# Gated cross-attention and a routed mixture of experts: the second group's experts chosen before the fourth group is mixed, and the fourth group's variances raised after the eighth scatter

## The reference, cut to what matters

```python
x = x + tanh(g_xattn) * (0.6 * sigmoid(si[:, :, None] + sj[:, None, :] + b) + 0.4 * layernorm(x))

xf = layernorm(x).reshape(-1, 256)
scores = sigmoid(xf @ w_router)                  # 32 experts in 8 groups of 4
sfc = scores + corr_bias
group_scores = top_k(sfc.reshape(T, 8, 4), 2)[0].sum(-1)
# the best 4 of the 8 groups are kept, and in them the best 6 experts
combine = scores at those 6 experts, else 0
g, u = xf @ gate_w[e], xf @ up_w[e]              # inner width 176
eo = (silu(g) * u) @ down_w[e]
routed = sum over e of combine[:, e] * eo[e]
shared = silu(xf @ sh_gate_w) * (xf @ sh_up_w) @ sh_down_w
x = x + tanh(g_ffn) * (routed + shared)
```

## Time and profile before

| | |
|---|---|
| median of 3 runs | 255.59 us (254.35 to 256.19) |
| span of the profiled execution | 256.1 us |
| TensorE matmul busy | 220.1 us (86%) |
| TensorE weight load busy | 172.2 us (67%) |
| VectorE busy | 130.3 us (51%) |
| ScalarE busy | 79.8 us (31%) |
| GpSimd busy | 147.0 us (57%) |
| moved by DMA | 53.32 MB, 208 GB/s over the span |
| chain that ended last | TensorE 69%, VectorE 13%, DMA 11% |

### The profile page before, as it was taken

How to read it: one execution, slowest core, us unless ns; L and a number is a source line. 1 busy time by engine, 2 the same in 40 slices (tenths; PEclk the granted TensorE clock), 3 DMA queues, 4 the chain that set the end, 5 groups by cost and what they waited for, 6 DMA issues and landing times.

```text
span 256.1 us, 5045 instructions
## 1 busy us (share of the span) xinstructions
PE 220.1 (86%) x1043; PEld 172.2 (67%) x1044; DVE 130.3 (51%) x528; ACT 79.8 (31%) x222; POOL 147.0 (57%) x139
## 2 busy tenths in 40 slices
PE   6896899996899986999999999999999998996000
PEld 5886687884667754877787777778777776774000
DVE  2598768989545542434444534444443443443344
ACT  3607022020011222343434344344444433433000
POOL 6226557777777742564675657656575665465500
PEclk9659599999799999999999999999999999999555
DMA  6999999999999989899785658767677675357787
GB/s 194 274 295 275 408 405 332 243 327 331 320 355 337 385 230 359 179 230 238 140 144 104 114 95 161 115 117 116 103 123 107 113 109 89 42 62 139 157 215 248
DMA packets 41016, 53.32 MB, mean 208 GB/s; under 512 B 5134, under 2 KB 35438, under 8 KB 40998
## 3 DMA queue, kind: packets, MB, share of 16 engines
q1 hardware_dynamic: 24944, 30.40, 40.3%
q0 software_dynamic: 11280, 17.99, 35.5%
q10 hardware_dynamic: 4774, 4.74, 7.1%
HBM read 31.72 MB, written 21.40 MB: 207 GB/s over the span
## 4 chain that ended last, share of the span: by engine, by line
PE 69%; DVE 13%; DMA 11%; issue 3%; POOL 1%; ACTq 1%; ACT 1%; SPq 0%; POOLq 0%
PE pG L734 25%; PE pY L748 17%; PE pG L673 5%; PE pX L728 5%; DMA sum_dram<-xnT,idx 5%; PE pH L742 4%; PE pG L757 4%; DMA xg<-rows_dram 3%; PE pY L684 3%; PE pY L776 3%; DMA given<-in_L_xattn_b_dram 2%; DMA wgu<-sum_dram 2%; PE pX L614 1%; DVE xs L900 1%; DVE rows L894 1%
## 5 line engine op out<-in xcount | busy, mean ns | idle before, releaser
L435 POOL DMA_INDIRECT sum_dram<-xnT,idx x56 | 87.1, 1556 | 61.6 <-ACT xnT L549 36.3
L734 PE MATMUL pG<-wgu,sdown 128*128 x224 | 76.1, 462 | 1.6 <-issue 1.1
L423 POOL DMA_INDIRECT rows_dram<-rows,row_i x48 | 47.2, 983 | 19.0 <-issue 13.8
L748 PE MATMUL pY<-wd,sup 88*128 x224 | 57.5, 379 | 0.0
L1122 DVE COPY sup<-pH 88x256 f32<-88x256 f32 x56 | 23.5, 420 | 58.0 <-PE pH L742 58.0
L734 PEld LDWEIGHTS pG<-wgu,sdown 128*128 128x128 f32 x224 | 38.4, 191 | 14.6 <-issue 2.6
L549 ACT ACTIVATE xnT<-pY,wt 128x256 f32<-128x256 f32 x56 | 26.6, 474 | 57.2 <-PE pY L748 24.7
L748 PEld LDWEIGHTS pY<-wd,sup 88*128 88x128 f32 x224 | 38.0, 190 | 3.2 <-issue 0.2
L742 PEld LDWEIGHTS pH<-ident,sgate 128*88 128x88 f32 x112 | 17.8, 161 | 13.6 <-issue 0.5
L542 ACT ACTIVATE sgate<-pG 128x176 f32<-128x176 f32 x56 | 17.8, 317 | 25.1 <-PE pG L734 24.6
L537 ACT ACTIVATE sdown<-pX 128x256 f32<-128x256 f32 x56 | 21.0, 377 | 7.4 <-PE pX L728 4.5
(11 more groups left out here) (181 smaller groups left out, 236.3 us busy)
## 6 DMA issues: line engine op xcount, KB each, us to landing
wgu<-in_L_ffn_gate_w_dram SPq DMA_DIRECT2D x8, 704.0 KB, 11.0
wgu<-in_L_ffn_up_w_dram SPq DMA_DIRECT2D x8, 704.0 KB, 11.7
wd<-in_L_ffn_down_w_dram SPq DMA_DIRECT2D x8, 640.0 KB
sum_dram<-zeros POOLq DMA_DIRECT2D x3, 1152.0 KB, 13.6
wgu<-sum_dram SPq DMA_DIRECT2D x12, 256.0 KB, 3.9
rows<-rows_dram ACTq DMA_DIRECT2D x16, 144.5 KB, 4.2
xg<-rows_dram ACTq DMA_DIRECT2D x16, 144.5 KB, 3.7
rows_dram<-zeros SPq DMA_DIRECT2D x8, 289.0 KB, 4.7
```

The source lines that it names most:

```text
L423: pool.indirect_dma_start(rows_dram[:, :], bass.IndirectOffsetOnAxis(ap=row_i[:, j, k:k + 1], axis=0), rows[:, j, :], None).then_inc(done, 16)
L435: pool.indirect_dma_start(sums_dram[into[s]][:, :], bass.IndirectOffsetOnAxis(ap=idx[:, s:s + 1], axis=0), y[s], None, compute_op=ALU.add) ...
L734: ins = nc.tensor.matmul(pG[par][:, 0:2 * M].rearrange("t (g m) -> t g m", g=2), xT[:, par, k, :], wgu[:, bass.ds(e, 1), :, k, :].rearrang ...
L748: ins = nc.tensor.matmul(pY[par][:, 0:H], hT[0:MI, par, i, :], wd[:, bass.ds(e, 1), i, :], start=(i == 0), stop=(i == I - 1))
```

## The change

On VectorE the second part's `choose_groups(1)` moves up behind `measure_group(2)`, its `bar_groups(1)` and `choose_experts(1)` behind `norm_group(2)`, and `choose_rows(1)` behind `shared_gate(3)`. On TensorE `places(1)` moves ahead of `shared_gate_up(3)`, with a wait for the second score instead of the third, and `shared_down(0)` now waits for the second `s_slot` instead of the first, which also keeps `router(2)` from writing before the places are read. On GpSimd `second_rstd(2)` stays behind the second scatter, and `second_rstd(3)` moves from behind the fourth to behind the eighth. The programs of ScalarE and SyncE are the same.

```diff
--- before
+++ after
@@ -439,8 +439,8 @@
                 for k in range(TOPK):
                     place(j, k)
-                    if j == 0 and k in (1, 3):
-                        second_rstd(2 + k // 2)
+                    if j < 2 and k == 1:
+                        second_rstd(2 + j)
@@ -694,16 +694,16 @@
             places(0)
             shared_gate_up(1)
             shared_gate_up(2)
+            pe.wait_ge(s_score, 2)
+            places(1)
             shared_gate_up(3)
             pe.wait_ge(s_sig, 2 * J)
-            pe.wait_ge(s_slot, 1)
+            pe.wait_ge(s_slot, 2)
             shared_down(0)
             router(2)
             shared_gate_up(4)
             router(3)
             shared_gate_up(5)
-            pe.wait_ge(s_score, 3)
-            places(1)
             shared_gate_up(6)
@@ -1032,21 +1032,21 @@
             shared_gate(0)
             mix_group(2)
             measure_group(2)
+            choose_groups(1)
             shared_gate(1)
+            norm_group(2)
+            bar_groups(1)
+            choose_experts(1)
             shared_gate(2)
-            norm_group(2)
             mix_group(3)
             measure_group(3)
             shared_gate(3)
+            choose_rows(1)
             norm_group(3)
             dve.wait_ge(s_x1, J)
             shared_add(0)
             find_busy()
-            choose_groups(1)
             shared_gate(4)
-            bar_groups(1)
-            choose_experts(1)
-            choose_rows(1)
             shared_gate(5)
             choose_groups(2)
```

## The result

The changed kernel takes 265.17 us (264.45 to 266.35, 4 runs) against 255.69 us (254.35 to 256.19, 4 runs) for the kernel before: ratio 1.0376, interval 1.0332 to 1.0420. A second set has 266.15 us (6 runs) against 256.89 us (16 runs): ratio 1.0394, interval 1.0329 to 1.0459. It is slower, as forecast, and by more than forecast: 9.3 to 9.5 us instead of 6.3, and outside the range. Each median is of all executions, and each ratio with its interval is of the fast ones alone, those no more than 1.5% above the fastest of their kernel, so the two can differ. The span of the profiled execution is 262.5 us, which is what the sum gave (262.35); that is luck, as its terms missed in opposite directions.

A forecast was written before the change was run, and what follows sets the result against it. VectorE and TensorE were both taken as full ahead of the table, on which the busiest expert waits. Span 256.1 + 8.5 (shift) - 2.25 (load) = 262.35 us, time 255.6 + 6.3 = 261.9 us; 8-in-10 range 257.5 to 264.2.

The forecast's parts named there:

- the sum: Whole kernel: span of 256.1 + 8.5 - 2.25 = 262.35 us, taken as a time of 261.9 us.
- TensorE has no cushion ahead of unit 6: Preparation: a wait put into TensorE ahead of unit 6 reaches the table one for one, less 0.35 us.
- the walk: Block-by-block timing of the new VectorE and TensorE order: idle 3.2 us before unit 3, 2.0 us before `shared_down(0)`.
- the GpSimd wait at the 25th scatter: Sign on GpSimd: it waits about 4.6 us there for the third slot, after gaining 2.7 us early.
- the shift: Preparation on TensorE: unit 6, the table and the busiest expert come 8.5 us later.
- the first rival: TensorE's clock stays up through one or both gaps: 258.5 us, or 259 to 260.5; chance 0.30, pure case 0.12.
- The clock rule of the Trainium skill: TensorE's new gaps: short idle gaps leave the clock up, longer ones lower it; by it this gap could still pass.
- With the scatters 6.5 us further ahead I take 5.0 us: 2.25 us back: Sixth tile's load: with scatters out earlier it takes 5.0 us instead of 7.25, giving 2.25 us back.
- The lower bound, 0: Sixth tile's load: nothing comes back, as the weights alone fill the DMA engines; the upper bound was 2.9 us.
- The row I leaned on (5.0 us): Kernel before: the load issued at 98.66 took 5.0 us with the scatters nearly through.
- slower than forecast: Rival: low clock lasts longer, 263.7 us, or later weights hold the tiles, 264.2 to 265.9 with nothing back; chance 0.12.
- the span lies 0.5 us above the median of the runs shown: Last step of the sum: turns the 262.35 us span into a time, 255.6 + 6.3 = 261.9 us.

The follow-up runs named there:

- run 4: Changed kernel with 12 and 7 spare matmuls keeping TensorE busy in its two new gaps; 262.66 us, ratio to before 1.0255.
- run 5: Changed kernel with unit 3 ahead of `places(1)` again and `choose_rows(1)` right behind unit 2's gate; 260.93 us, ratio to before 1.0233.
- run 1: The kernel before, run again with no edit; 258.42 us against 257.73 us, ratio 1.0024.
- run 11: The changed kernel, run again with no edit; 266.15 us against 256.89 us for the kernel before.
- run 7: The kernel before with the last three weight parts held until the fourth tile's first matmuls are done; 257.97 us, ratio 1.0081.
- run 3: The changed kernel without GpSimd's part, group 3's variances staying behind the fourth scatter; 265.16 us.
- run 8: The kernel before with group 3's variances raised behind the sixth scatter instead of the fourth; 256.78 us against 256.98 us, ratio 1.0065.
- run 6: The kernel before with 10 and 13 spare matmuls in its own two long TensorE gaps; 255.13 us against 256.98 us, ratio 0.9904.
- run 10: The kernel before with 10 and 13 spare matmuls in TensorE's gaps and the sixth tile's load issued behind the fifth's; 257.64 us against 256.89 us, ratio 0.9876.

## Why the prediction was right and where it was wrong

**Right: TensorE has no cushion ahead of unit 6.** Both waits came at the foretold places: 2.89 us for `chosen_b` (3.2 by the walk) and 2.09 us for the second slot (2.0). `find_busy` ended at 47.36 (foretold near 48), the GpSimd wait at the 25th scatter was 5.57 us (4.6), the busiest expert started at 77.39 (near 79), and runs 4 and 5 moved the loss by taking these waits' effects away. One row was read wrongly, without a price: the largest gap of TensorE between 34.46 and 45.01 is not the 0.35 us but 0.38 us ahead of `router(3)`, at 41.71.

**Right, slightly too large: the shift.** The term was 8.5 us; unit 6 came 7.6 us later, 8.0 if counted from the first counting, and the busiest expert 7.5 to 8.0 us. Unit 3 was taken wholly at the low level, 4.17 us from its start to its gate; it took 3.75 (35.55 to 39.30), as the clock rose under its last rows. That rise was part of the first rival (259 to 260.5 us), but it gave only 0.4 us, since the clock fell again under `shared_down(0)`. The clock rule of the Trainium skill (TensorE: Matmul & The Clock Gate, Part 1: The HAM clock gate), by which short gaps leave the clock up, would have given 5.2 us. The rows decide against it for gaps of this length: behind 2.89 us the clock fell, and in run 1 behind 2.66 us.

**Wrong: "With the scatters 6.5 us further ahead I take 5.0 us: 2.25 us back".** This is the step that failed. The load took 6.92 us in the profiled execution (6.73 in run 11), and the second distance shrank by 0.3 us (145.4 against 145.7). The scatters did end earlier beside TensorE's work, by 4.9 us rather than 6.5 (17.5 us behind the start of the busiest expert instead of 22.4), but the load was hardly quicker for it: in run 11 all of them had landed ahead of it, and it took 6.73 us, whereas run 7 left them and held the weights, and it fell to 3.2 us. The last weights wait for the busiest expert's end, so they move with TensorE, and the load meets them in the changed kernel as before. The row I leaned on (5.0 us) I read as quick for want of scatters. It was issued 7.3 us behind the last of the weights, and in run 7, with no scatters, the loads become quicker in the same way as the weights run out. The lower bound, 0, was the value, and with it the forecast is 255.6 + 8.5 = 264.1 us. That is the low end of the rival "slower than forecast" ("with nothing back 264.2 to 265.9"), whose chance was 0.12 and in which the measured time lies; of its conditions this one came, and a longer low level did not. By the Trainium skill's rule of taking turns between the queues (DMA: Bandwidth & Descriptors, Queues, rings and completion order) the load was to take an estimated 4.8 us. The trace does not agree, as one queue fell silent and the load sped up by 0.3 us only. Why weights on one queue hold a small load on another for so long, no run shows.

**Wrong: "the span lies 0.5 us above the median of the runs shown".** The span was set beside the time as if they were one measure. The time is 1.9 us above the span, so the profiled execution took 258.0 us and lay 2.4 us above the shown median. By its own step the sum is 256.1 + 6.25 + 1.9 = 264.3 us, beside 264.45 for the profiled execution of the changed kernel. The agreement is luck: the 6.4 us between the two spans are 7.5 us more in the first distance, less 0.3 in the second, less 0.4 by which the first counting came earlier, less 0.4 behind the last matmul, and the last two stand in no term of the sum. The median of the three runs shown was also 1.3 to 2.5 us below the later ones, which my range, 257.5 to 264.2, did not allow for.

**Open.** The medians differ by 9.3 us, the profiled executions by 5.1 to 6.6. Each profiled execution of the changed kernel was the lowest of its set, and the two of the kernel before were not. Of the 9.3 us, 7.5 to 8.0 are shown as the preparation by the first profiles, and 8.3 by the means of five and three. Where the other 1 to 2 us come from is not shown; run 3's profile points at both stages.

## What to carry to other kernels

Filling a waiting engine's gap with work from further on is only free if the engine that feeds it does not get a new wait: list the waits that move on every engine, and walk the loop between them once before counting the filled gap as a gain. A stage that ends with one engine waiting for another may still have no slack earlier, if they meet in between. When a transfer was quick, list all that was under way beside it, and since when, before crediting one neighbour that had ended. Compare spans with spans and times with times, and take a median of three runs as no firmer than the spread of the kernel.

## What the runs showed of the hardware

- The time of a run lies 1.8 to 2.0 us above the span of the same run (264.45 and 262.5, 258.48 and 256.6, 251.67 and 249.8).
- A gap on TensorE of 2.66 us in the tiles (run 1) was followed by a granted clock low enough to make four matmuls take 2.71 instead of 1.45 us; one of 1.76 us in the kernel before was not. The length of the gap alone does not decide: one of 1.77 us in run 4 was followed by 2.68 us for the four matmuls, and one of 2.15 us in run 8 by 1.45 us.
- 10 and 13 spare matmuls in gaps of 2.6 and 3.0 us took 4 us off the preparation of the profiled execution (39.8 us in runs 6 and 10, 42.1 to 43.9 without them); the median of run 6 was 1.9 us lower, that of run 10 was not.
- A tile load of 145 KB took 7.25 us beside freshly issued weight parts and the last scatters, 6.73 us beside the weights with all scatters landed (run 11), and 3.2 us just behind the last scatter with the last weights held (run 7).
